# A gated delta-rule layer on one core: where updates and preparations stand between a state's transposes and its reads

## The reference

```
Sk  = einsum('bhvk,bhk->bhv', S, k_t)
S   = a_t[..., None] * S - (b_t[..., None] * (Sk - v_t))[..., None] * k_t[:, :, None, :]
o_t = einsum('bhvk,bhk->bhv', S, q_t)
```

## Time and profile before

| what | value |
|---|---|
| median of three runs | 2928.49 us (2927.63 to 2932.69) |
| the profiled execution | 2931.77 us, span on the core 2930.0 us |
| TensorE busy, share of the span | 77% |
| VectorE busy | 66% |
| ScalarE busy | 45% |
| GpSimd busy | 19% |

### The profile page before, as it was taken

The page is one execution under the profiler, slowest core; times in us unless marked ns, Lnnn a source line. Parts: engine busy times, 40 slices in busy tenths (PEclk is TensorE's granted clock), DMA queues, the critical chain, the costliest instruction groups (busy, mean ns, idle before and its releaser), DMA issues.

```text
span 2930.0 us, 67669 instructions
## 1 busy us (share of the span) xinstructions
PE 2243.2 (77%) x24976; PEld 1691.7 (58%) x24976; DVE 1919.4 (66%) x4412; ACT 1319.4 (45%) x2752; POOL 559.3 (19%) x546
## 2 busy tenths in 40 slices
PE   5999888888863777677777777777776776399998
PEld 3455666666653666666666666666666665234443
DVE  4223777777773777777777777777777777523334
ACT  2002666666661534454454445445444543044434
POOL 0000333333333212212221221122122212200000
PEclk9999999999986978988897888889789878599999
DMA  5001444555555333333333333343333333301110
GB/s 216 7 13 38 192 188 193 200 200 206 207 207 190 114 104 131 125 110 106 130 115 106 131 122 116 99 135 112 111 128 121 114 100 117 140 33 72 72 57 22
DMA packets 139483, 358.77 MB, mean 122 GB/s; under 512 B 11312, under 2 KB 92968, under 8 KB 126424
## 3 DMA queue, kind: packets, MB, share of 16 engines
q1 hardware_dynamic: 139176, 354.92, 34.1%
q0 software_dynamic: 48, 0.16, 0.0%
HBM read 226.97 MB, written 128.07 MB: 121 GB/s over the span
## 4 chain that ended last, share of the span: by engine, by line
PE 48%; issue 20%; ACT 12%; DVE 11%; POOL 6%; DMA 3%; DVEq 0%; SPq 0%; POOLq 0%; ACTq 0%
PE PS L1306 9%; ACT arena L680 5%; PE PS L1412 4%; PE PS L1439 4%; PE PS L1294 3%; PE PS L1345 3%; ACT arena L685 3%; PE PS L1169 3%; PE PS L1217 3%; PE PS L1320 3%; POOL arena L487 2%; PE PS L1333 2%; DMA arena<-beta_d 2%; PE PS L1265 2%; PE PS L1233 2%
## 5 line engine op out<-in xcount | busy, mean ns | idle before, releaser
L1192 PE MATMUL PS<-arena 128*128 x2048 | 491.0, 399 | 98.8 <-DVE arena L886 97.9
L886 DVE SCALAR_TENSOR_TENSOR arena<-PS,SM,arena 128x256 f32<-128x256 f32 x1152 | 468.6, 476 | 124.9 <-ACT arena L596 122.2
L1192 PEld LDWEIGHTS PS<-arena 128*128 128x128 f32 x2048 | 395.8, 195 | 194.0 <-DVE arena L886 114.0
L1306 PE MATMUL PS<-arena 128*128 128x128 f32 x1920 | 312.0, 311 | 113.1 <-ACT arena L685 109.5
L1306 PEld LDWEIGHTS PS<-arena 128*128 128x128 f32 x1920 | 262.4, 212 | 156.7 <-ACT arena L685 151.3
L525 POOL TENSOR_TENSOR arena<-arena 128x256 f32<-128x256 f32 x128 | 98.6, 770 | 1265.4 <-DVE arena L985 1265.4
L680 ACT ACTIVATE arena<-arena 128x128 f32<-128x128 f32 x960 | 302.1, 395 | 0.0
L929 DVE TENSOR_TENSOR arena<-arena,PS 128x512 f32<-128x512 f32 x192 | 127.5, 685 | 246.7 <-PE PS L1345 246.6
L596 ACT ACTIVATE arena<-PS,SM 128x256 f32<-128x256 f32 x384 | 207.6, 565 | 152.3 <-PE PS L1192 148.7
L660 ACT COPY arena<-PS 128x512 f32<-128x512 f32 x154 | 90.2, 586 | 411.5 <-PE PS L1233 195.5
L1294 PE MATMUL PS<-ident,arena 128*128 128x128 f32 x960 | 171.2, 307 | 31.0 <-ACT arena L680 30.7
(11 more groups left out here) (138 smaller groups left out, 3871.6 us busy)
## 6 DMA issues: line engine op xcount, KB each, us to landing
arena<-g_d SPq DMA_DIRECT2D x128, 512.0 KB, 4.2
vas_d<-arena SPq DMA_DIRECT2D x24, 2048.0 KB, 6.9
arena<-vas_d SPq DMA_DIRECT2D x128, 384.0 KB, 3.4
kq_d<-arena SPq DMA_DIRECT2D x8, 4096.0 KB, 11.4
arena<-kq_d SPq DMA_DIRECT2D x16, 2048.0 KB, 9.4
arena<-beta_d SPq DMA_DIRECT2D x8, 2048.0 KB, 8.1
kb_d<-arena SPq DMA_DIRECT2D x8, 2048.0 KB, 13.9
arena<-kb_d SPq DMA_DIRECT2D x16, 1024.0 KB, 6.4
```

Of the source, the lines that this page charges most:

```text
L886: nc.vector.scalar_tensor_tensor(acc, raw[:, :, i:i + PT_], CW[:, w, i, hh:hh + 1], acc, ALU.mult, ALU.add).then_inc(job_free if i == TAPS ...
L1192: ins = mm(dst.rearrange("p (b n) -> p b n", b=B), W4[:, w, kt, DH * h:DH * (h + 1)], XNT[:, kt, :, bass.ds(c * PT_ + (HALO - halo), halo ...
L1306: ins = mm(bank(7)[:, 128 * gi:128 * (gi + 1)].rearrange("v (l x) -> v l x", l=NB), STR[:, s % 2, gi, :], KQ[d][:, :, p0:p0 + 2].rearrange ...
```

## The change

In blocks with three slots TensorE's order becomes: T(first), update, R(first), T(second), prep 0, R(second), T(third), prep 1, R(third). The same instructions are issued. On ScalarE the decay of the third slot comes directly behind the first slot's `state_copy`, ahead of the first `read_copy`; the copies of preparations (`next_evac`) stand behind the second and the third slot's `state_copy` instead of the first and second. Blocks with two slots keep their order on both engines. VectorE, GpSimd and the DMA queue keep theirs everywhere.

```diff
@@ ScalarE, blocks of a chunk @@
                         if k == 0 and len(reads) > 1:
                             decay(reads[1])
                         state_copy(s)
-                        if k < 2:
+                        if k == 0 and len(reads) > 2:
+                            decay(reads[2])
+                        if k > 0 or len(reads) < 3:
                             next_evac()
-                        if 0 < k < len(reads) - 1:
-                            decay(reads[k + 1])
                         read_copy(s)
@@ TensorE, blocks of a chunk @@
                     preps = list(enumerate(items_of(m, nxt)))
-                    for u in U_AT[m] if nxt else []:
-                        if u not in (1, 4):
+                    fill = [u for u in U_AT[m] if u not in (1, 4)] if nxt else []
+                    if len(reads) < 3:
+                        for u in fill:
                             update(u)
-                    for k, s in enumerate(reads):
+                        fill = []
+                    for s in reads:
                         state_transposes(s)
-                        if preps:
+                        if fill:
+                            update(fill.pop(0))
+                        elif preps:
                             prep(m, *preps.pop(0))
                         reads_of(s)
```

## The result

The changed kernel takes 2849.45 us (median of 4, 2844.69 to 2852.84), the kernel before beside it 2929.05 us (4 runs, 2927.63 to 2932.69). The ratio is 0.9725, with a 95% interval of 0.9708 to 0.9743: 80 us less. The forecast was 2854, within 2825 to 2884.

A forecast was written before the change was run, and what follows sets the result against it. VectorE, idle 15.8 us a chunk waiting for TensorE's `corrections`, showed the bound. Blocks 2, 3, 4 and 6 gave 1.7 + 0 + 3.3 + 0 = 5.0 us a chunk, 75 us over 15 chunks: 2854, range 2825 to 2884.

The forecast's parts named there:

- Block 2: Third slot's waits for its decay and for the copy go away on TensorE; 1.72 us a chunk saved.
- The rule weighed there: Weight loads overlap only across row groups: one exposed load at four places in blocks 2 and 4, 0.8 us a chunk, 2866.
- Block 4: Reads and transposes move ahead of TensorE's 4.61 us wait for VectorE; 3.3 us a chunk saved, 4.9 if the clock stays up.
- the 2.2 us read from one chunk: Block 4: the clock fell 2.2 us after TensorE idled; about 3 us idle remains, so the slow 3.3 was taken.
- Block 3: First read is set by ScalarE and stays; saved 0, at worst -0.2 us a chunk.
- the rival that had the half clock in block 3: Half clock outlasts block 2 into block 3; 7.0 us cost against 5.0 saved, 2958, chance 0.03.
- a sign of being wrong: Granted clock lying elsewhere in blocks 2 to 4, or a first read there starting later relative to `corrections`.
- Block 6: The 1.44 us ScalarE wait moves from R(12) to R(13); saved 0, bounds 0.6 us gain to 0.3 us loss.
- The clock up in block 4: Rival: full clock stays behind block 4's wait; 6.6 us a chunk in all, 2830, chance 0.22.
- The clock rising later in block 2: Rival: half clock lasts to block 2's end, which then gives nothing; 3.3 us a chunk, 2879, chance 0.2.
- Unchanged: Rival: VectorE is the bound and gives the time back, or block 4's reads are held; 2928, chance 0.03.
- slower: Rival: half clock outlasts block 2 and covers block 3; 2.0 us a chunk lost, 2958, chance 0.03.

The follow-up runs named there:

- e1: Changed kernel with the new order on TensorE and ScalarE in block 4 alone, the old one elsewhere; 2876.81 us, ratio 0.9813 to the kernel before.
- e5: Changed kernel with the new order on TensorE and ScalarE in blocks 3 and 6 alone, the old one elsewhere; 2932.37 us, ratio 1.0008 to the kernel before.
- e3: Changed kernel with ScalarE's new order kept and TensorE's old order everywhere; 2882.18 us, ratio 0.9833 to the kernel before.
- f1: Changed kernel with TensorE's old order in blocks 3 and 6, ScalarE's new order everywhere; 2829.75 us, ratio 0.966 to the kernel before.
- f2: Changed kernel with all three reads of block 4 ahead of its preparations and their copies; 2829.35 us, ratio 0.9656 to the kernel before.
- e2: Changed kernel with the new order on TensorE and ScalarE in block 2 alone, the old one elsewhere; 2885.64 us, ratio 0.986 to the kernel before.
- e4: Changed kernel with the third slot's decay back behind the preparation's copy on ScalarE, except in block 6; 2902.32 us, ratio 0.9903 to the kernel before.
- f3: Changed kernel with the edits of f1 and f2 together; 2785.64 us, ratio 0.9509 to the kernel before.
- g1: f3 with block 3's second decay behind its first state copy on ScalarE; 2783.93 us, ratio 0.9498 to the kernel before.
- h1: f3 with four unused identity matmuls in front of block 1's update, where TensorE waits; 2774.37 us, ratio 0.9475 to the kernel before.
- h2: Changed kernel with nine unused identity matmuls in block 4's wait in front of preparation 0; 2874.2 us, ratio 0.9801 to the kernel before.

## Why the prediction was right, and where only its sum was

**Block 2: right.** Forecast 1.72 us a chunk; step 3 fell by 1.62, by 1.4 in the short and 2.1 in the long chunks, and by 1.38 with block 2 alone. In the short chunks the clock rises at 1535.4, so the slow stretch holds R(0) and the first preparation, as it did before, and all of T(1): T(1) takes 0.99 us (1532.66 to 1533.65) where it took 0.78 (1570.63 to 1571.41), and that is 0.2 of the 0.35 missing. In the long ones the clock rises ahead of that preparation, which is why they gain more here. Both waits vanished as described, and the update covers the first copy. The rule weighed there does not show: R starts 1.44 us behind the start of its preparation and is 0.99 us long, where the rows of before gave 1.46 and 1.00. The Trainium skill, "TensorE: Matmul & The Clock Gate", section "The mechanism", says that weight loads overlap running matmuls only where the row group differs; this trace does not agree. The full-height loads of R(2) start 0.11 us apart, each while the matmul in front of it (0.28 us long in the profile) still runs, and the 0.2 us that one exposed load would have cost is not there.

**Block 4: mechanism right, size between the two forecasts.** I took 3.3 with the old place of the half clock and gave 4.9 if the clock stayed up. Step 5 fell by 4.20 (3.64 alone). The half clock is there, as forecast, in 11 of 14 chunks, but half as long: in chunk 6 R(7) is 1.30 us from start to start instead of 1.87, and T(8) 0.54 instead of 0.80. From the end of preparation 0 to `corr_transposes` it is 6.24 - 1.96 = 4.28 us for 5.13 forecast, and 0.57 + 0.26 of these 0.85 come from those two. In the three chunks in which the clock stayed up, step 5 is 5.0 us shorter than before in two and 4.9 in the third, the 4.9 forecast for that case. The reason given for the slow value does not hold, though: the same wait of 2.85 us is followed by a fall 2.1 us after its start in the short chunks, 2.6 in the long ones, 3.9 in e1, with TensorE busy again for 1.0, and by none in those three. So the 2.2 us read from one chunk do not tell whether the clock falls.

**Block 3: right at the full clock, wrong with the half clock on it.** In the chunks of the short kind step 4 is 14.15 to 14.25, close to the 14.09 of before: the forecast zero, less 0.1. In the five long ones it is 15.78, and in e5, where nearly every chunk has the half clock on R(3), 15.58. The step that failed reads "`key_mask` of preparation 1 on VectorE comes about 0.1 us later; block 4's idle time of 0.57 us hides that". A row of VectorE in a long chunk:
```profile
1647.48 0.42 DVE L894 TENSOR_TENSOR arena<-PS,mask 128x256 f32<-128x256 f32 x1 [1.41 <-PE PS L1255]
```
This wait occurs once in each of the five long chunks and in no other (7.0 us together). It arises inside block 3, in VectorE's own order, so the idle time in front of block 4 can't take it. Averaged, block 3 costs 0.66 us a chunk. It is a small form of the rival that had the half clock in block 3, and a half clock elsewhere in blocks 2 to 4 is what the prediction named as a sign of being wrong. What the old order would lose with the half clock on R(3) was not seen: the eight traced kernels with TensorE's old order in block 3 have none there in any of their 112 chunks, the five with the new one in 37 of 70. So how much of the 1.5 us is the order's and how much the clock's is open, but in these runs the half clock on R(3) came only with the new order.

**Block 6: right.** Step 7 is 10.95 against 10.90. The wait stands in front of R(13) as forecast, with 1.44 us. What the prediction did not see is that the change pays for this zero: ScalarE's half alone is worth 1.4 us a chunk there (e3, f1).

**The clock elsewhere.** Step 2 lost 0.42 us with nothing edited in blocks 0 and 1. The sum is 1.62 + 4.20 - 0.66 + 0 + 0.42 = 5.6 us a chunk, with the other steps 5.66, against 5.0 forecast; block 4's surplus of 0.9 and step 2's 0.42 made good for block 3. The total was close partly by luck: errors of both signs lay in it.

**The rivals.** The clock up in block 4 (2830) came about in full in three chunks and by half in the others. The clock rising later in block 2 (2879) did not come about: counted in work it rose at most one T later, in the short chunks, and not at the block's end. Unchanged and slower are refuted. VectorE's idle times came at 3.38 and 2.40 us for 3.0 and 3.2, block 4's wait at 2.85 for 3.

## What to carry to other kernels

When work is moved to cover a wait, look who consumes what was moved at a fixed place of its own order: undoing in blocks 3 and 6 the TensorE edit that gained in 2 and 4 saved 20 us more (f1). Where a wait for another engine stands in the middle of a block, put everything that doesn't need it ahead, not only what fits by count: f2 took another 2.0 us out of block 4. And where edits also move the clock, time combinations: two that gave 20 us each gave 64 together, and one that removed a wait cost 25.

## What the runs showed of the hardware

**Chunk lengths settle on common values.** e1, e2 and e3 shorten different waits by different amounts, yet 13 of the 14 chunks of each take 98.94 to 99.06 us. The kernel before (102.34 to 102.46) and e5 (102.33 to 102.42) share a value too, and so do f1 (95.52 to 95.58) and f2 (95.51 to 95.69); the last of the 14 is up to 2 us longer in all of them. Windows of e3, one chunk apart, where the granted clock has the same place in each:
```profile
1534.00:1540.00 6.00, 4.01 (x110) 0.53 0.48 160
...
1546.00:1563.00 17.00, 15.30 (x292) 0.84 0.27 79
...
1633.00:1640.00 7.00, 5.00 (x115) 0.52 0.46 150
...
1645.00:1662.00 17.00, 15.30 (x293) 0.84 0.26 79
```
A loop whose half clock returns at the same place in every turn keeps its length, and an edit moves it to another such pattern; in the changed kernel two patterns take turns. This would explain why gains did not add up (53 and 45 us gave 80, 20 and 20 gave 64). It is argued from these tables; no run fixed the clock to show it, and it does not cover all of them: the chunks of e4 take 99.1 to 102.8 us, those of f3 and g1 91.9 to 93.9, of h1 89.3 to 93.2, of h2 97.0 to 99.7.

**The price of the half clock shows inside one kernel.** The chunks of a kernel run the same instructions in the same order. In the changed kernel step 5 is 11.5 us with the full clock in block 4, and 12.4 to 12.7 with a half clock of 3.4 us there. In h1 step 3 is 9.44 us where R(0) has the full clock, and 12.9 to 13.2 in nine chunks where it has not.

**More TensorE work can make the kernel faster or slower.** Four unused matmuls in block 1 gave 11 us back (h1), and nine in block 4 cost 25 us (h2).
